# A graph network kernel: six beats of preparation a superblock, early products from superblock 14, both parts in one matmul

## The reference

```python
h = jnp.maximum(_layernorm(x, axis=-1), 0.0)
x = x + _L0_gnn_ref(h, edge_index, W1, b1, W2, b2, W3, b3)   # three graph convolutions
h = jnp.maximum(_layernorm(x, axis=-1), 0.0)
x = x + _L1_gnn_ref(h, relvectors, w_ih, w_hh, b_ih, b_hh, src, dst, edge_type_16)

def conv(h, W, b):                                  # norm = dinv[src] * dinv[dst]
    h = h @ W
    agg = jax.ops.segment_sum(h[src] * norm, dst, num_segments=n)
    return agg + b
# the second block: msg = h[src] + relvectors[rel], summed by destination, then one GRU cell
```

## Time and profile before

| | us |
|---|---|
| median of 3 runs | 930.28 |
| lowest, highest | 929.97, 931.42 |
| profiled execution | 930.96 |
| its span, first to last instruction | 926.9 |
| PE busy | 885.6 |
| DVE busy | 443.9 |
| ACT busy | 290.0 |
| POOL busy | 75.6 |

### The profile page before, as it was taken

How to read it: one execution, slowest core, us unless ns; L and a number is a source line. 1 busy time by engine, 2 the same in 40 slices (tenths; PEclk the granted TensorE clock), 3 DMA queues, 4 the chain that set the end, 5 groups by cost and what they waited for, 6 DMA issues and landing times.

```text
span 926.9 us, 16603 instructions
## 1 busy us (share of the span) xinstructions
PE 885.6 (96%) x5495; PEld 529.5 (57%) x5495; DVE 443.9 (48%) x1164; ACT 290.0 (31%) x609; POOL 75.6 (8%) x244
## 2 busy tenths in 40 slices
PE   2779999999999999999999999999999999999997
PEld 1348777777777865444444544444464455555554
DVE  6956888888888211021112414444344133333346
ACT  3365566666666311011111212222232122112212
POOL 0210102000000015552000000000000000000000
PEclk9979999999999999999999999999999999999999
DMA  6100000000000310000000101111401001000001
GB/s 192 30 2 1 4 17 17 22 16 16 17 22 16 122 55 2 3 2 1 1 0 24 43 8 46 46 46 46 143 19 31 1 28 30 23 23 23 23 24 42
DMA packets 37008, 28.50 MB, mean 31 GB/s; under 512 B 12869, under 2 KB 35553, under 8 KB 36924
## 3 DMA queue, kind: packets, MB, share of 16 engines
q1 hardware_dynamic: 36252, 26.97, 9.6%
q10 hardware_dynamic: 672, 0.41, 0.2%
HBM read 17.56 MB, written 9.81 MB: 30 GB/s over the span
## 4 chain that ended last, share of the span: by engine, by line
PE 92%; DVE 4%; ACT 1%; issue 1%; SPq 0%; DMA 0%; DVEq 0%
PE ps L1246 42%; PE ps L911 13%; PE ps L813 10%; PE ps L1257 5%; PE ps L640 4%; PE ps L643 4%; PE ps L1276 2%; PE ps L648 2%; PE ps L651 2%; PE ps L892 2%; PE ps L860 1%; DVE node_b L920 1%; PE ps L848 1%; PE ps L880 1%; PE ps L627 1%
## 5 line engine op out<-in xcount | busy, mean ns | idle before, releaser
L1246 PE MATMUL ps<-count,node_b 128*128 128x512 f16 (+3 forms) x1400 | 270.5, 351 | 0.4 <-DVE node_b L1408 0.3
L813 PE MATMUL ps<-node_b 128*128 128x175 f16 x808 | 193.5, 260 | 13.2 <-issue 8.2
L1246 PEld LDWEIGHTS ps<-count,node_b 128*128 128x128 f16 (+2 forms) x1400 | 121.4, 97 | 142.2 <-issue 7.3
L911 PE MATMUL ps<-node_a,count 128*128 128x256 f16 x1050 | 200.6, 277 | 0.2 <-DVE node_a L1032 0.2
L920 DVE TENSOR_TENSOR node_b<-node_b 128x1024 f16<-128x1024 f16 (+2 forms) x303 | 161.8, 587 | 0.0
L1115 ACT ACTIVATE count<-ps 128x500 f32 x202 | 122.8, 608 | 96.4 <-PE ps L813 94.7
L1246 PE MATMUL ps<-count,node_a 128*128 128x512 f16 (+2 forms) x700 | 134.7, 352 | 0.0
L813 PEld LDWEIGHTS ps<-node_b 128*128 128x128 f16 x808 | 79.7, 99 | 62.4 <-issue 27.0
L911 PEld LDWEIGHTS ps<-node_a,count 128*128 128x128 f16 x1050 | 101.2, 100 | 4.0 <-ACT count L1115 0.4
L1246 PEld LDWEIGHTS ps<-count,node_a 128*128 128x128 f16 (+1 forms) x700 | 60.0, 97 | 73.9 <-issue 7.1
L1338 DVE SCALAR_TENSOR_TENSOR work<-ps,dinv,params 128x256 f32<-128x256 f32 (+1 forms) x25 | 12.0, 480 | 125.0 <-PE ps L1257 125.0
(11 more groups left out here) (210 smaller groups left out, 789.0 us busy)
## 6 DMA issues: line engine op xcount, KB each, us to landing
node_a<-in_x SPq DMA_DIRECT2D x4, 768.0 KB, 8.5
table_scratch<-agg SPq DMA_DIRECT2D x21, 128.0 KB, 1.8
node_b<-table_scratch SPq DMA_DIRECT2D x3, 768.0 KB, 6.5
xt<-x_scratch SPq DMA_DIRECT2D x16, 128.0 KB, 2.2
out<-scaled SPq DMA_DIRECT2D x16, 128.0 KB, 1.7
xt<-in_x SPq DMA_DIRECT2D x12, 128.0 KB, 2.0
params<-in_x SPq DMA_DIRECT2D x12, 128.0 KB, 2.1
x_scratch<-xt SPq DMA_DIRECT2D x12, 128.0 KB, 1.7
```

Source lines behind the costliest of these rows:

```text
L813: return PE.matmul(window(s)[:, :, keys], low, key_hot[k][:, j, :, i].rearrange("p (t w) -> p t w", w=SPAN), start=(s == 0 and j == 0), st ...
L911: last = PE.matmul(out_slot(u)[0:m, :], count[:, t, u * P:u * P + m], node_a[:, t, part, :], start=(t == 0 and part == 0), stop=(t == T - ...
L1246: last = PE.matmul(ps[:, b, 0:cols], nodes[0:k, t, part, f * P:(f + 1) * P], count[0:k, t, c * CHUNK:c * CHUNK + cols], start=(n == 0 and ...
```

## The change

- Six beats go with a superblock, not four. The beats' places move: counts 23, multiply 26, histogram 30 (a beat of its own), scale steps 32, weighting 36, factors 38, low part 12 beats behind the weighting.
- Early products begin at superblock 14, not 18. Both parts of a source tile go in one matmul of 512 columns (`node_a[:, t, :, :]`), so the two halves of the sum lie side by side in a bank, and `out_bias_dve` adds them in two steps. The matmuls after the build (L1276) are joined too. Within a superblock the products stand behind quarter 0, behind quarter 1, and between the carry and the last source matmul.
- The first pair's rows are made by DVE before and just behind the verdict.
- Carry rows are made for four superblocks at a time.
- Offset words are loaded in five loads: 11 as before, 8 at the start, 7, 7 and 8 at superblocks 2, 4 and 6.
- ACT's shaping stands 3 superblocks behind the sum (5 before), DVE's low part 12 (9 before).
- POOL clears the last tile's table before its first self loops.

```diff
-OFFSET_LOADS, LAST_WORDS_AT = (11, 18, 12), 4
+OFFSET_LOADS, WORDS_AT = (11, 8, 7, 7, 8), (2, 4, 6)
...
-BEATS = 4
+BEATS = 6
...
+        carry_hot = [piece(flat_b, GROUP * T).rearrange("p (m k i) -> p m k i", m=GROUP // 2, i=2) for _ in range(2)]
...
+        def rank_and_source_rows(m):
+            k, two = m % PAIRS_KEPT, slice(BATCH * m, BATCH * (m + 1))
+            one_hot(rel_rank_hot[BATCH * m // GROUP % 2][:, :, m % 2, :, :], rel_rank_k[:, :, two], 0, WINDOW).then_inc(*dve_seq.up())
+            one_hot(low_hot[k], low_k[:, :, two], 0, P).then_inc(*dve_seq.up())
+            if m % 2 == 0:
+                n = min(GROUP, NS - BATCH * m) // 2
+                one_hot(carry_hot[BATCH * m // GROUP % 2][:, 0:n, :, :],
+                        carry_k[:, BATCH * m:BATCH * m + 2 * n].rearrange("p (m i) -> p m i", i=2), 1, T).then_inc(*dve_seq.up())
+
+        def key_rows(m):
+            one_hot(key_hot[m % PAIRS_KEPT], key_k[:, :, BATCH * m:BATCH * (m + 1)], 0, T * SPAN).then_inc(hot_made, 1)
...
             DVE.tensor_reduce(verdict[:, :], rules, AX_X, ALU.add).then_inc(verdict_summed, 1)
+
+            DVE.wait_ge(keys_out, 5)
+            rank_and_source_rows(0)
             DVE.wait_ge(judged, 1)
             DVE.tensor_copy(verdict_i[:, :], ps[0:1, 5, 0:1]).then_inc(verdict_in, 1)
+            key_rows(0)
...
-        COUNTS_AT = 24
+        COUNTS_AT = 23
...
+        HIST_AT = 30
+        WEIGHT_AT = 26
+        SCALE_AT = 32
         DEGREE_AT = 36
-        WEIGH_AT = 40
-        FACTORS_AT = 42
+        WEIGH_AT = 36
+        FACTORS_AT = 38
         AHEAD_ACT = 2
-        LOW_PART_AT = WEIGH_AT + 8
-        OUT_AT, OUT_LOW_AT = 5, 9
+        LOW_PART_AT = WEIGH_AT + BATCH * BEATS
+        OUT_AT, OUT_ACT_AT, OUT_LOW_AT = 5, 3, 12
...
-        PRODUCTS_FROM = (WEIGH_AT + T) // BEATS + 2
-        early_products = [(u, t, part) for u in range(EARLY) for t in range(T) for part in range(2)]
-        LAST_PRODUCTS = 24
+        PRODUCTS_FROM = max((WEIGH_AT + T) // BEATS + 2, SETTLE_FIRST + 3)
+        early_products = [(u, t) for u in range(EARLY) for t in range(T)]
+        LAST_PRODUCTS = 12
...
         def out_slot(u):
-            return ps[:, OUT_BANK + u % OUT_SLOTS, 0:D]
+            return ps[:, OUT_BANK + u % OUT_SLOTS, :]
...
                         next_keys = span_of(s, j + 1)
-                        for u, t, part in between[len(between) * j // QUARTERS:len(between) * (j + 1) // QUARTERS]:
-                            early_product_pe(u, t, part)
+                        if j < QUARTERS - 2:
+                            between_pe(between, j)
                     else:
...
                             relations_pe(s // GROUP)
+                        between_pe(between, QUARTERS - 2)
                         sources().then_inc(win_done, 1)
...
-            last = PE.matmul(out_slot(u)[0:m, :], count[:, t, u * P:u * P + m], node_a[:, t, part, :],
-                             start=(t == 0 and part == 0), stop=(t == T - 1 and part == 1), skip_group_check=True)
+            last = PE.matmul(out_slot(u)[0:m, :], count[:, t, u * P:u * P + m], node_a[:, t, :, :].rearrange("p a d -> p (a d)"),
+                             start=(t == 0), stop=(t == T - 1), skip_group_check=True)
...
-            DVE.scalar_tensor_tensor(out=work[k][0:m, :], in0=out_slot(u)[0:m, :], scalar=newt[0:m, 1, u:u + 1], in1=xt[1][0:m, :],
+            DVE.scalar_tensor_tensor(out=scaled[k][0:m, :], in0=out_slot(u)[0:m, D:2 * D], scalar=newt[0:m, 1, u:u + 1], in1=xt[1][0:m, :],
+                                     op0=ALU.mult, op1=ALU.add).then_inc(*dve_seq.up())
+            DVE.wait_ge(*dve_seq.now)
+            DVE.scalar_tensor_tensor(out=work[k][0:m, :], in0=out_slot(u)[0:m, 0:D], scalar=newt[0:m, 1, u:u + 1], in1=scaled[k][0:m, :],
                                      op0=ALU.mult, op1=ALU.add).then_inc(conv_read, 1)
...
-                    if s == summed_at[u] + OUT_AT:
+                    if s == summed_at[u] + OUT_ACT_AT and summed_at[u] + OUT_AT < NS:
                         out_shape_act(u)
...
+            POOL.wait_ge(x_weighted, T)
+            POOL.memset(node_a[:, T - 1, :, :], 0.0).then_inc(tail_cleared, 1)
             POOL.wait_ge(ident16_made, 1)
             for u in range(EARLY):
                 POOL.wait_ge(win_written, settled(u))
                 loops(ALU.add, u, u + 1, POOL).then_inc(tile_looped, 1)
-                if u == 0:
-
-                    POOL.wait_ge(x_weighted, T)
-                    POOL.memset(node_a[:, T - 1, :, :], 0.0).then_inc(tail_cleared, 1)
```

More of the change, by code:

```diff
@@ L801, in build_pe @@
                 between = due if s + 1 < NS else []
+                if s in WORDS_AT:
+                    offset_words.extend(load_offsets(2 + WORDS_AT.index(s)))
                 PE.wait_ge(hot_made, s // BATCH + 1)
@@ L830, in build_pe, with between_pe @@
                         beside_pe(w)
-                if s == WEIGHT_AT // BEATS + 1:
-                    PE.wait_ge(hist_due, 2)
-                    for w in range(WINDOW):
-                        for q in range(Q):
-                            part, pair = divmod(w, WINDOW // 2)
-                            last = PE.matmul(HIST, low_of[q][part][0:lanes(q), pair // 2, :, pair % 2],
-                                             high_of[0:lanes(q), (q * WINDOW + w) // 2, :, w % 2],
-                                             start=(w == 0 and q == 0), stop=(w == WINDOW - 1 and q == Q - 1), skip_group_check=True)
-                    last.then_inc(degrees_done, 1)
-                for u, t, part in due[len(between) * (QUARTERS - 1) // QUARTERS:]:
-                    early_product_pe(u, t, part)
+                for u, t in due[len(between):]:
+                    early_product_pe(u, t)
+        def between_pe(products, j):
+            for u, t in products[len(products) * j // (QUARTERS - 1):len(products) * (j + 1) // (QUARTERS - 1)]:
+                early_product_pe(u, t)
         def relations_pe(g):
@@ L893, in beside_pe @@
                 last.then_inc(x_weighted, 1)
+            if beat == HIST_AT:
+                PE.wait_ge(hist_due, 2)
+                for w in range(WINDOW):
+                    for q in range(Q):
+                        part, pair = divmod(w, WINDOW // 2)
+                        last = PE.matmul(HIST, low_of[q][part][0:lanes(q), pair // 2, :, pair % 2],
+                                         high_of[0:lanes(q), (q * WINDOW + w) // 2, :, w % 2],
+                                         start=(w == 0 and q == 0), stop=(w == WINDOW - 1 and q == Q - 1), skip_group_check=True)
+                last.then_inc(degrees_done, 1)
             if beat == COLUMNS_AT:
@@ L900, in beside_pe, with early_product_pe @@
                 last.then_inc(abs_summed, 1)
-        def early_product_pe(u, t, part):
+        def early_product_pe(u, t):
             m = rows(u)
-            if t == 0 and part == 0:
+            if t == 0:
                 PE.wait_ge(win_written, settled(u))
@@ L1274, in layers_pe @@
                 for t in range(T):
-                    for part in range(2):
-                        last = PE.matmul(out_slot(u)[0:m, :], count[:, t, u * P:u * P + m], node_a[:, t, part, :],
-                                         start=(t == 0 and part == 0), stop=(t == T - 1 and part == 1))
+                    last = PE.matmul(out_slot(u)[0:m, :], count[:, t, u * P:u * P + m], node_a[:, t, :, :].rearrange("p a d -> p (a d)"),
+                                     start=(t == 0), stop=(t == T - 1))
                 last.then_inc(conv_done, 1)
```

40 lines of the change are left out of this document (20 added, 20 removed).

## The result

| | before | changed |
|---|---|---|
| median of 15 runs each, us | 930.78 | 933.99 |
| lowest, highest | 929.91, 931.74 | 931.43, 935.02 |
| span of the profiled execution | 926.9 | 929.7 |

The changed kernel is slower: 1.0033 times the time of before, 95% interval 1.0026 to 1.004. Forecast were 919.5 us and a range that ended at 931. It is rival B's case: the superblock kept its old length.

The account below looks back on a forecast made before the run. PE's path was taken as the bound, its sequencer pacing superblocks: 98 us preparation + 1.9 (clock) + 188 x 1.06 = 299.2 against 309.96. With 0.4 from late tiles, span 915.7, forecast 919.5 us, range 910.5 to 931.

Parts of the forecast that it names:

- rival B: Steady part: gaps don't depend on the number of products, a superblock stays at 1.143 us, 935 us in all; chance 0.11.
- The steady part: Early products beside superblocks: wider products cover the gaps before register-fed sources, 1.06 us a superblock instead of 1.143.
- break-even of 1.12: Steady part: the us a superblock at which the change would neither gain nor lose time.
- Joint parts: Products of 512 columns for pairs of 256: 2 us by columns, the rest from covered gaps before register-fed sources.
- DVE: Steady part: DVE needs 1.024 us a superblock, the two-step output adding 0.056, and no longer waits 23.5 us for ACT.
- floor of 1.02: Steady part: the shortest superblock held possible, 1.02 us, set by DVE's work.
- Rival C: Steady part: DVE becomes the bound or both engines trip over each other, 1.10 us a superblock, 927 us; chance 0.14.
- Start: Preparation: PE starts about 24.3 us after a shorter offset load; second pair's rows come at 33.0 us against 31.4.
- The new wait (c): Preparation: later maxima push the all-reduce to 61.1 us; PE stands 3.5 us for the fourth pair's rows before superblock 6.
- rival A: Preparation: the all-reduce's 5.6 us don't follow the wait; superblock 14 begins at 94.5 us, 916 us in all; chance 0.20.
- "98": End of the preparation: superblock 14, the first with products, begins at 98 us (94.5 to 102).
- Rival D: Preparation: longer PE idle times hold its clock low through the weighting; superblock 14 at 102 us, 923.5 in all; chance 0.15.

Follow-up runs that it names:

- e4: Changed kernel with each source tile's product split again into two matmuls of 256 columns and a one-step bias; 934.88 us.
- e7: Kernel before, with PE's wait for DVE's rows (hot_made) asked only at the first superblock of each pair; 919.24 us.
- e11: Kernel before, with PE's wait for a written window (win_written) moved from the first source matmul to the carry matmul; 910.32 us.
- e5: Changed kernel with both PE waits (pair's rows, and written window for one window more) at even superblocks only; 930.93 us.
- e9: Changed kernel with PE's wait for a written window (win_written) moved from the first source matmul to the carry matmul; 910.65 us.
- e2: Changed kernel with the source matmuls' columns fixed, so no register steps and counts in wrong columns; waits kept; 910.49 us.
- e1: Changed kernel with POOL's first self loops put before its clear of the last tile's table again; 929.82 us.
- e13: e9 with a wait on a long-met semaphore (verdict_in) added at each superblock's first source matmul; 934.06 us.
- e14: e9 with a wait on a long-met semaphore (verdict_in) added beside win_written at the carry matmul; 934.81 us.
- e12: Changed kernel with a third wait, on a long-met semaphore (verdict_in), at each superblock's first source matmul; 934.42 us.

## Why the prediction was wrong, step by step

**The steady part, the step that failed.** The gaps were rightly found before register-fed source matmuls, and rightly put to PE's sequencer. Wrong was how long the sequencer needs: "all it had in 1.143 was 0.17 for 5.58 pairs" took the bare 0.97 us of the earlier trace rows as its base, from superblocks 0 and 1. These have no second wait. With it a bare superblock takes 1.13 us, and one with its products 1.139: the sequencer was busy for the whole length, products cost it next to nothing (e4), and neither fewer of them nor their place as cover could win time. The kernel before was bound in the same way (e7, e11). The list of PE's queue showed 199 semaphore instructions in it; no step asked for them. The term was 1.06 and came out at 1.139, 14.9 us over 188 superblocks.

**Rival B** had the right time (935 against 933.99) and the right mechanism in its words, "register-fed sources cost what they cost", though not the part that could be removed. Its break-even of 1.12 fits e5, which had 1.118 and took 930.93 us. It had 0.11, because a gap behind one narrow product was read as missing cover.

**Joint parts.** By columns 0.01 us a superblock: the pace went from 1.143 to 1.139, and e4 puts the edit at 0.9 us, not told apart from none. The forecast had 188 x (1.143 - 1.06), 15.6 us, for the steady part. What it had worked out from the Trainium skill (TensorE: Matmul & The Clock Gate, section "Wait — 56ns, not 53.3ns?"), an estimate of under 1.5 us in the whole build, was nearer. The second step of the bias takes 9.1 us for 19, 477 ns each, as bounded.

**DVE.** 1.024 us a superblock predicted; in the changed kernel DVE was busy 167.30 us from 104 to 290 us, 1.02 for each. e9, in which PE has no gaps, runs at 1.014 with DVE busy for 180.10 of 186 us, 0.98 each. So the size was right, and the floor of 1.02 nearly so; the wait for ACT went as said. Rival C did not come.

**Start.** 24.3 us predicted, 24.11 measured; the second pair's rows 33.0, measured 32.00; counts 54, measured 52.57.

**The new wait (c), wrong, as rival A had it.** The maxima ended at 54.37 us, as the order had told (55.5), but the all-reduce came 1.0 us later, not 5.6:

```profile
L1553 POOLq MODIFY_POOL_CONFIG  x2: 4/4/4, 49.8 to 49.8; - x2
L1553 POOL PARTITION_ALL_REDUCE fours<-bounds x1: 386/386/386, 55.4 to 55.4; - x1
```

The configuration stands at 49.8, before the wait, and 5.6 us pass from there to the operation; in the kernel before they were 5.8 (50.7 to 56.53). e2 settles that they run beside the wait and don't follow it: its maxima ended at 53.52 us, and the all-reduce came at 56.15, 2.6 us later, but again some 5.6 us behind its configuration at 50.5. The Trainium skill (GPSIMD Engine Reference, section "2.1 Instruction dispatch") counts its 6 us from that instruction too, but less the wait for events. The traces agree on the size and not on the subtraction: the changed kernel's 5.6 us hold a wait until 54.37. PE stood 2.57 us, not 3.5, before superblock 6, and the first weighting product came at 64.14 us, not 69, the last tile at 88.97 to 90.04, not 94.5. That is some 5 us better than forecast, and rival A's 94.5 for superblock 14 would have been near: its first source ran at 93.55.

**POOL's way back, seen by nobody.** The change list named the clear before the first self loops, and no step priced it. It cost 4.31 us of PE, of which e1 gave back 4.2, and it cancelled (c): 98.10 us against "98" was luck, two errors of opposite sign. The granted clock fell to 0.65 and 0.50 around it (stretches of 4 us):

```profile
94.00:98.00 4.00, 0.00 (x0) 0.00 (x0) 2.73 (x6) 0.40 (x1) 0.41 (x1) 0.65 0.00 0
98.00:102.00 4.00, 3.90 (x19) 2.16 (x20) 0.00 (x0) 0.59 (x1) 0.00 (x1) 0.50 0.01 4
102.00:106.00 4.00, 4.00 (x36) 2.80 (x35) 3.57 (x7) 2.49 (x5) 0.05 (x1) 1.00 0.02 3
```

**Rival D** did not come: the clock was 0.50 from 58 to 66 us and 0.76 from 66 to 70, no longer low than in the kernel before (0.53, 0.50 and 0.69 from 62 to 74) and 4 us earlier.

**Altogether.** Without POOL's wait the change is worth 0.1% (e1, 0.9979 to 0.9997). Of the forecast's 11 us no more than 5.1 showed even with the extra instruction gone and POOL's order mended: the old design then runs in 910.32 and the new one in 905.20.

## What to carry to other kernels

Where an engine waits for nobody and still has gaps, list its queue and count every kind of instruction in it, semaphore instructions too; a matmul that waits for two semaphores costs one more of them, so where the sequencer is the bound ask for each wait at the matmul that needs it. A bare reference row ("the same work with nothing beside it") must have the same waits as the place that it is applied to. And where GpSimd changes between library calls and ordinary operations, put the first instruction of the other kind where the engine is idle.

## What the runs showed of the hardware

- A second wait on a matmul becomes an EVENT_SEMAPHORE instruction in its queue, 51 ns by the record, which cost 0.10 us (superblocks 0 and 1) to 0.13 us each (superblock 12 to 13) though its semaphore had long been met (e13, e14); a third wait brought no further one (e12). With the register steps gone, 199 of them left no gap (e2).
- Taking some 200 of these away was worth 23.3 us of 934 (e9), and about 20 us of the kernel before (e11).
- The register instructions that work out a matmul's columns started 0.10 us apart with records of 36 to 53 ns; three sources fed by them made a bare superblock of 1.00 us (e9), and 0.38 with fixed columns (e2).
- GpSimd's all-reduce came 5.6 us behind its configuration whether its input was ready 1.0 us (changed kernel) or 2.6 us (e2) before it.
- GpSimd's way back from the all-reduce to a tensor operation took 6.9 us (90.70 to 97.59), starts with its configuration and can be hidden; a memset ran before it without it.
- After 4.31 us in which PE stood, the granted clock was 0.50, 1.2 GHz, for the next stretch of 4 us; without that wait (e1) it was 1.00 throughout 90 to 102 us.
